# Batch 0 of a routed expert kernel: rows fetched by slot through a table made on TensorE, in place of rows scattered to their slots

## What is computed

```python
def _time_mix_layer(x, ln_w, ln_b, Wk, Wv, Wr, Wo):
    normed = _layer_norm(x, ln_w, ln_b)
    kv = (normed @ Wk.T) * (normed @ Wv.T)
    state = DECAY * state + (1.0 - DECAY) * kv_t          # along the tokens
    return x + (sigmoid(normed @ Wr.T) * states) @ Wo.T
x = _layernorm(x + attn(x))                               # two such layers
top_k_logits, expert_indices = top_k(x @ router_w + router_b, 2)
expert_inputs = zeros(E, cap, C).at[expert, pos].add(x)   # rows by slot
h = expert_inputs @ w_c_fc + b_c_fc;  g = expert_inputs @ w_gate + b_gate
o = silu(h * g) @ w_c_proj + b_c_proj
out = _layernorm(x + sum over k of prob[k] * o[expert[k], pos[k]])
```

## Time and profile before

| what | us |
|---|---|
| median of three timed runs | 365.52 (362.71 to 366.84) |
| span of the profiled execution | 382.6 |
| PE busy in it | 332.7 (87%) |
| DVE busy | 262.8 (69%) |
| POOL busy | 203.9 (53%) |
| ACT busy | 166.2 (43%) |

### The profile page before, as it was taken

How to read it: one execution, slowest core, us unless ns; L and a number is a source line. 1 busy time by engine, 2 the same in 40 slices (tenths; PEclk the granted TensorE clock), 3 DMA queues, 4 the chain that set the end, 5 groups by cost and what they waited for, 6 DMA issues and landing times.

```text
span 382.6 us, 7195 instructions
## 1 busy us (share of the span) xinstructions
PE 332.7 (87%) x2338; PEld 292.0 (76%) x2338; DVE 262.8 (69%) x853; ACT 166.2 (43%) x302; POOL 203.9 (53%) x244
## 2 busy tenths in 40 slices
PE   6889975869999999999999999877799986997880
PEld 3555653669879789997888999877689886987870
DVE  6688895787668868787787798831437684675225
ACT  2644434436545445555454445432435443363200
POOL 4185078850345642244557668377554437764752
PEclk9999896969999999999999999996999999898996
DMA  8949743150131133111114532222256111111152
GB/s 207 207 58 203 186 147 119 59 140 2 32 100 36 50 87 99 35 48 33 38 37 174 150 100 54 61 75 62 61 138 121 37 42 51 23 47 40 28 153 69
DMA packets 61246, 32.61 MB, mean 85 GB/s; under 512 B 15995, under 2 KB 58823, under 8 KB 61210
## 3 DMA queue, kind: packets, MB, share of 16 engines
q1 hardware_dynamic: 55322, 23.43, 25.3%
q0 software_dynamic: 4256, 7.94, 7.2%
q10 hardware_dynamic: 1632, 0.79, 0.7%
HBM read 19.01 MB, written 13.69 MB: 85 GB/s over the span
## 4 chain that ended last, share of the span: by engine, by line
PE 67%; issue 9%; DVE 8%; POOL 7%; another core or an unknown queue 3%; DMA 3%; ACT 3%; POOLq 0%; DVEq 0%; ACTq 0%
PE ps_o L795 20%; POOL slot_rows L1495 3%; PE pair0g L780 3%; PE pair0g L778 3%; PE pair1g L778 3%; PE bank L756 3%; PE bank L639 2%; PE pair1g L780 2%; PE bank L649 2%; PE pair0g L779 2%; PE bank L619 2%; PE pair1g L779 2%; PE bank L651 2%; PE pair1h L778 2%
## 5 line engine op out<-in xcount | busy, mean ns | idle before, releaser
L795 PE MATMUL ps_o<-proj_sb,hidden 128*104 128x128 f32 x768 | 99.7, 279 | 4.2 <-DVE o_sb L1311 2.1
L795 PEld LDWEIGHTS ps_o<-proj_sb,hidden 128*104 128x104 f32 x768 | 93.3, 175 | 5.8 <-issue 5.4
L1495 POOL DMA_INDIRECT slot_rows<-x_rows,row_to x64 | 72.5, 1133 | 45.1 <-DVE prod L1299 25.8
L1547 POOL DMA_INDIRECT picked<-expert_rows,row_from x48 | 49.9, 1039 | 37.4 <-DVE prod L1299 24.3
L984 ACT ACTIVATE gate_s<-pair0g,bgate_sb 128x308 f32<-128x308 f32 x64 | 33.1, 517 | 81.8 <-PE pair0g L780 52.7
L1299 DVE SCALAR_TENSOR_TENSOR prod<-pair1h,bfc_sb,gate_s 128x308 f32<-128x308 f32 x64 | 34.0, 532 | 32.3 <-ACT gate_s L984 17.7
L1299 DVE SCALAR_TENSOR_TENSOR prod<-pair0h,bfc_sb,gate_s 128x308 f32<-128x308 f32 x64 | 34.2, 534 | 26.4 <-ACT gate_s L984 11.8
L991 ACT ACTIVATE hidden<-prod 128x616 f32<-128x616 f32 x64 | 45.6, 712 | 7.7 <-DVE prod L1299 7.7
L984 ACT ACTIVATE gate_s<-pair1g,bgate_sb 128x308 f32<-128x308 f32 x64 | 33.0, 515 | 33.8 <-PE pair1g L780 22.2
L778 PE MATMUL pair1g<-slotT_hi,gate_hi 128*128 128x308 f32 x64 | 26.6, 416 | 10.0 <-DVE prod L1299 4.9
L1512 POOL DMA_INDIRECT returned<-o_sb,home x21 | 21.6, 1029 | 17.3 <-DVE prod L1299 11.2
(11 more groups left out here) (233 smaller groups left out, 773.0 us busy)
## 6 DMA issues: line engine op xcount, KB each, us to landing
slot_in<-slot_rows SPq DMA_DIRECT2D x20, 260.0 KB
expert_rows<-o_sb SPq DMA_DIRECT2D x24, 156.0 KB
x_in<-in_L_attn_h SPq DMA_DIRECT2D x4, 512.0 KB, 5.7
x_rows<-in_L_ffn_w_gate SPq DMA_DIRECT2D x8, 256.0 KB
x_rows<-in_L_ffn_w_c_fc SPq DMA_DIRECT2D x8, 256.0 KB
proj_sb<-in_L_ffn_w_c_proj SPq DMA_DIRECT2D x8, 256.0 KB, 5.3
out<-picked SPq DMA_DIRECT2D x12, 128.0 KB, 2.6
slot_rows<-slot_in SPq DMA_DIRECT2D x5, 260.0 KB, 7.2
```

The source lines that it names most:

```text
L795: mm = nc.tensor.matmul(ps_o[0:PART, P * part:P * part + P], hidden[:, e % 2, c, PART * part:PART * part + PART], proj_sb[:, e, c, :], sta ...
L1495: nc.gpsimd.indirect_dma_start(out=slot_rows, out_offset=bass.IndirectOffsetOnAxis(ap=row_to[:, c:c + 1], axis=0), in_=x_rows[:, b, c // K ...
L1547: nc.gpsimd.indirect_dma_start(out=picked[:, j, k, :], out_offset=None, in_=expert_rows[b % 2], in_offset=bass.IndirectOffsetOnAxis(ap=row ...
```

## The change

For batch 0 alone, the scatter and the load of slots are replaced:

- SP writes the normed rows of batch 0 to a DRAM tensor `first_rows` in two DMAs, behind the loads of `proj_sb`.
- DVE (stage `map`) splits `row_to` into a block (row / 128) and a lane (row mod 128) and compares both with constant number lists: `in_block`, 128x320, and four `in_lane`, 128x512 each. POOL (`weigh`) multiplies `in_block` by the token numbers, in two instructions. PE (`map`) multiplies `in_lane` with these, 16 matmuls of 128x40 in bfloat16 into `ps_o`: the token number of every slot. DVE (`picks`) adds the two halves of it into `slot_token`.
- POOL (`fetch`) gathers each of the five groups with four indirect DMAs of 128 rows of 512 bytes from `first_rows` into the ring `slot_in`, 20 DMAs in all. POOL gets four more small constants at the start.
- The first pair no longer waits for all of the head. `out` of batch 1's last step moves into period 0 behind the first pair; slot groups 1 and 2 are transposed at points 1 and 7; the splitting of the weights of experts 4 to 7 (`high`, `low`) moves from the head to points 1 to 14 of period 0; the stages of `..._ROUTE` and `..._MIX` come one point later in period 0, and so do the scatters of batch 1. Four filler matmuls are put ahead of `kvr` of batch 1's third step.

```diff
+SCALAR_FIRST = {0: [("added", 1, 3)], 1: [("high", 4, 0), ("high", 4, 1)], 3: [("high", 5, 0), ("high", 5, 1)],
+                8: [("high", 6, 0)], 9: [("high", 6, 1)], 11: [("high", 7, 0)], 13: [("high", 7, 1)]}
+VECTOR_FIRST = {0: [("stats", 1, 5)], 3: [("low", 4, 0), ("low", 4, 1), ("stats", 2, 0)],
...
+SLOT_TURNS_FIRST = {1: (0, 1), 7: (0, 2), 8: (0, 3), 19: (0, 4), 28: (1, 0), 29: (1, 1), 30: (1, 2)}
...
+def stages_at(table, b, point):
+    if later(b):
+        return table.get(point, [])
+    return table.get(point - 1, []) + (table.get(point, []) if point + 1 == POINTS else [])
...
+            for half in range(2):
+                sp.wait_ge(normed_made[1], step(0, 4 + half))
+                sp.dma_start(first_view[:, HT * half:HT * half + HT, :], x_ln[:, 0, HT * half:HT * half + HT, :])\
+                  .then_inc(first_stored, 16)
...
-            load_slots(0, range(GROUPS))
...
+            def slot_map(b, _):
+                pe.wait_ge(blocks_weighed, 2)
+                for c in range(K * TILES):
+                    if c % 4 == 0:
+                        pe.wait_ge(lanes_made, c // 4 + 1)
+                    mm = nc.tensor.matmul(ps_o[:, 0:2 * BLOCKS], in_lane[:, P * c:P * c + P],
+                                          weighed[:, c, :, :].rearrange("p w h -> p (w h)"),
+                                          start=(c == 0), stop=(c == K * TILES - 1))
...
                 if c == 0 and not later(b):
-                    for read in (r_copied, k_copied, kv_made):
+                    for read in (r_copied, k_copied):
                         pe.wait_ge(read, nth(1, 4, 4))
-                    pe.wait_ge(rows_made, 1)
-                    pe.wait_ge(pool_low_made, 2 * LOW_BY_POOL)
-                    pe.wait_ge(vector_low_made, 2 * (E - LOW_BY_POOL))
-                    pe.wait_ge(x_added, step(1, 3))
...
+                for i in range(4):
+                    nc.vector.tensor_tensor(in_lane[:, 4 * P * i:4 * P * i + 4 * P].rearrange("p (c l) -> p c l", l=P),
...
+                                            .to_broadcast([P, 4, P]), ALU.is_equal).then_inc(lanes_made, 1)
...
+            def fetch(b, g):
+                if g == 0:
+                    pool.wait_ge(map_copied, 2)
+                    pool.wait_ge(first_stored, 16 * 2)
+                    pool.wait_ge(rows_zeroed, 16 * GROUPS)
+                if g >= SLOT_RING:
+                    pool.wait_ge(slots_turned, g - SLOT_RING + 1)
+                for i in range(4):
+                    nc.gpsimd.indirect_dma_start(
+                        out=slot_x[:, g % SLOT_RING, i, :], out_offset=None, in_=first_rows,
+                        in_offset=bass.IndirectOffsetOnAxis(ap=slot_token[:, 4 * g + i:4 * g + i + 1], axis=0),
```

More of the change, by code:

```diff
@@ L106 @@
+FILL = {("weights", 0, 0): 12, ("turn", 0, 0): 1, ("turn", 0, 3): 3, ("turn", 0, 4): 6, ("turn", 0, 5): 2, ("count", 0, 0): 6,
+        ("kvr", 1, 2): 4}
 TENSOR_MIX = {9: [("turn", 0)], 10: [("kvr", 0)], 12: [("turn", 1)], 13: [("kvr", 1)], 14: [("out", 0)],
@@ L171, in scatters_at @@
         return [n for n in range(K * TILES) if SCATTER_FROM + 3 * n // 4 == point]
-    return [n for n in range(K * TILES) if SCATTER_FROM + n == point]
+    return [n for n in range(K * TILES) if SCATTER_FROM + n + (not later(b)) == point]
 def nth(b, per, k):
@@ L739, in turn_slots @@
                     pe.wait_ge(rows_made, b + 1)
-                if g == 2:
+                if g == 1 and not later(b):
+                    pe.wait_ge(k_copied, mixed - 1)
+                if g == 2 and later(b):
                     pe.wait_ge(kv_made, mixed)
@@ L743, in turn_slots @@
                     pe.wait_ge(logits_copied, nth(b, 2, 2))
+                if g == 2 and not later(b):
+                    pe.wait_ge(logits_copied, nth(1, 2, 2))
                 if g < 2 and later(b):
@@ L857, in period @@
                     hidden_pair(b, e, j)
+                    if not later(b):
+                        for name, of, n in TENSOR_FIRST.get(point, ()):
+                            stages[name](of, n)
                     if b == LAST:
@@ L1008, in period @@
                     gate_copy(b, e, j)
+                    if not later(b):
+                        for name, of, n in SCALAR_FIRST.get(point, ()):
+                            stages[name](of, n)
                     if b == LAST:
@@ L1414, in period @@
                     product(b, e, j)
-                    if point in SLOT_TURNS:
-                        ahead, g = SLOT_TURNS[point]
+                    if not later(b):
+                        for name, of, n in VECTOR_FIRST.get(point, ()):
+                            stages[name](of, n)
+                    if point in slot_turns(b):
+                        ahead, g = slot_turns(b)[point]
                         if b + ahead < B:
@@ L1532, in low_of @@
                                         ALU.subtract).then_inc(pool_low_made, 1)
-            stages = {"rstd": rstd_of, "shares": shares, "scatter": scatter_tile, "low": low_of}
+            stages = {"rstd": rstd_of, "shares": shares, "weigh": weigh, "fetch": fetch, "low": low_of}
             def gather(b, c):
```

188 lines of the change are left out of this document (132 added, 56 removed).

## The result

The changed kernel takes 373.62 us (median of 4, 371.59 to 376.05) against 366.18 of the kernel before, timed beside it on the same chip: a ratio of 1.0235, with a 95% interval of 1.0182 to 1.0287. I had predicted 364.5, within 1%, so the prediction is wrong in size and in sign. A second set of runs gives 372.98 and 1.0213 (1.0172 to 1.0253).

The account below looks back on a forecast made before the run. TensorE was taken to bound period 0, after a gap before its first pair. A 5.6 us earlier first pair, shrunk to 1.6 by DVE's queue, left 1.0: 365.5 - 1.0 = 364.5 us, range 360.0 to 368.6.

Parts of the forecast that it names:

- The table and fetches: Head: `kv` at 50.9, `weigh` 0.5 to 2 and hidden, gathers 1.45 each, group 0 issued at 60.8, needed at 73.
- Rival C: POOL: gathers cost 2.15, delaying the first pair and `rstd` of batch 2; slower by 4 to 5, 370; chance 0.08.
- The first pair, 76.85: End of the head: the first pair starts at 76.85, 5.6 earlier than 82.46, with DVE ending the wait.
- rival B: Low TensorE clock behind the gap 57.9 to 63.3: first pair 2 to 4 later, whole 366.5 to 368.5; chance 0.2.
- kvr (2.58 ...), to 69.1: TensorE in the head, behind `carry` and four fillers: `kvr` takes 2.58 and ends at 69.1.
- DVE from product 0 to product 9, 20.6: Period 0: 18.6 of DVE work plus 2 of waits, product 9 at 98.8; the lead shrinks from 5.6 to 1.6.
- From pair 8 on: Later period 0: pair 12 at 105.4 against 106.36, then TensorE has most to do; gain 0.9 to 1.
- The sum: Whole kernel: span 382.6 - 1.0 = 381.6, carried to the median as 365.5 - 1.0 = 364.5.
- Rival A: Period 0: DVE does not hold TensorE, pair 12 at 100.95; gain 5.4, 360.1; chance 0.24.
- the likeliest case: Period 0: DVE's queue holds TensorE with waits of 0 to 4; 362.5 to 366, chance 0.48.

Follow-up runs that it names:

- e9: e3 with both `rstd` ahead of the gathers, the slots' low part ahead of the head's last `stats`, only 4 fillers, ahead of the first pair: 362.14 us, ratio 0.9940.
- e1: Changed kernel plus 12 filler matmuls ahead of the transposes in the head and 10 ahead of the first pair: median 371.35 us, no ratio.
- e3: Changed kernel with the fillers of e1 and the early splits and statistics of e2: 364.79 us, ratio 1.0001 to the kernel before.
- e4: Kernel before with only the table, gathers and stores of rows in place of the scatters and load: 370.71 us, ratio 1.0154.
- e8: e4 with the `high` and `low` splits reordered, `high` of expert 4 behind `added` and `turned`: 368.41 us, ratio 1.0110.
- e10: Changed kernel, unchanged, run again with more rounds: 372.98 us, ratio 1.0213 to the kernel before.
- e5: Changed kernel with only the two `stats` of batch 2's first step moved to the head: 370.42 us, ratio 1.0132.
- e6: Changed kernel with only expert 4's split (two `high`, two `low`) moved to the head: 369.99 us, ratio 1.0114.
- e2: Changed kernel with expert 4's split and the two `stats` of batch 2's first step both moved to the head: 368.41 us, ratio 1.0114.

## Why the prediction was wrong, by its steps

- **The table and fetches.** Right in its times, in part by luck. `kv` was expected at 50.9 and started at 50.73, `picks` ended in time, and no transpose waited for a gather. But `weigh` took 3.1 (48.25 to 51.39), over its bound of 2, and TensorE waited 0.93 for it; nothing came of that, because `picks` stands behind the scan. The 23.1 us for 15 scatters are 1.54 each, not the 1.45 taken; gathers came every 1.30, except behind a slow one. That group 0 was issued by 60.65 (60.8 forecast) is the sum of one gather of 2.07 and three of 1.00. Rival C did not come: no `norm` waited behind the last eight gathers. Its second half was hardly tested here, since DVE came to `norm` of batch 2 only at 106.28, with `rstd` ready at 98.4; once the rest is faster it shows (0.36 in e9). The first gather started 0.27 within a scan; of the others four took 1.16 to 1.53, one of them (1.53) started within a `low`, and a gather that started with a scan (72.16, the scan at 72.15) took 1.00. For C, 0.7 would have been needed on each of 20; in all the twenty took 22.2 where 20 times 1.00 is 20. The rule of the Trainium skill (SBUF — State Buffer, "Who interferes with whom"), that a VectorE instruction with two SBUF inputs contends with a GpSimd instruction that reads SBUF, agrees with the two slowest of these and not with the one at 72.16.

```profile
L1646 POOL DMA_INDIRECT slot_in<-first_rows,slot_token x20: 992/999/2072, 54.7 to 96.0; - x20
```

- **The first pair, 76.85.** Measured 80.28. `norm` started at 62.12 as forecast (62.15); then the granted clock was 0.50 over the `carry`, the fillers and part of `kvr`. That is rival B, with its place and its price (2 to 4 us later, 79 to 81). The fillers show it: without the cold stretch 3.0 us come back. Counted from `row_to`, the first pair was forecast 29.1 behind and came 33.0 behind; of the 0.9 that the clock does not explain, half lies ahead of `norm` and half behind it. The step that failed is "kvr (2.58 ...), to 69.1" at full clock: the prediction had the half-clock stretch behind the old gap in its rows, saw the new gap, and still gave this 0.2.

- **DVE from product 0 to product 9, 20.6.** This is the step that turned a gain into a loss. Measured 26.59 (82.23 to 108.82). The work was counted right, the waits were not: one window over this stretch,

```profile
82.23:108.82 26.59, 21.09 (x148) 19.84 (x148) 18.61 (x83) 13.11 (x26) 12.53 (x16) 0.85 0.21 61
```

  has DVE busy for 18.61 us against 18.6 in the sum, and so 7.98 us of waiting where I took 2 and allowed 4. With the head's clock kept up (e1) it is 5.7, and with splits and `stats` early as well (e3) 3.3:

```profile
78.57:102.82 24.25, 18.75 (x146) 17.49 (x146) 18.51 (x83) 13.11 (x26) 12.53 (x16) 0.93 0.23 66
```

```profile
80.28:98.64 18.36, 16.69 (x146) 15.75 (x146) 15.05 (x64) 12.01 (x24) 12.44 (x16) 1.00 0.23 59
```

  So DVE's queue did not just hold TensorE: each held the other in turn, through the copy of the slots on ScalarE and through the bank of `logits`. The prediction added up one engine's queue and took the others' answers as ready.

- **From pair 8 on.** The prediction said that "the work done by then is the same in both" and gave the rest of the period no cost at all. Pairs 8 to 12 take 0.84 more, of which 0.56 is a wait for a product (at 108.36), and 12 to 32 take 1.46 more. It is almost the same in every version that keeps the change's order (11.07 for the first piece in e9, where POOL's `rstd` adds 0.36), and nothing in the two that have the old one (e4, e8). In e3 TensorE waits 0.63, 0.65 and 0.50 in the second piece, where before it waits 0.26 and 0.54. Which of the later stages, the splits of experts 6 and 7 or the shift by a point, makes these was not tried.

- **The sum.** Against the kernel before, pair 32 is 9.99 us later in the recorded profiles: first pair -2.58, pairs 0 to 6 +4.00, 6 to 8 +6.27, 8 to 12 +0.84, 12 to 32 +1.46. The timed medians differ by 7.4, as the profiled execution was the longest of its four (376.05). Of the 6.27, 1.6 went with the clock (11.03 to 9.42 in e10), 2.9 with the `stats` ahead of the first `top` (9.42 to 6.48 in e5, which takes away the wait of 1.88 and the low clock that e10 still has behind it), 0.9 with the splits (to 5.62), and 0.9 stays.

- **Rival A** is excluded: DVE held TensorE more than in the likeliest case.

The chance of a loss over 1% was 0.11, from C and the end of B. What was missed is that B does not stop at one place: behind the waits for DVE's queue the low clock came back, in this profile twice more (at the first pair and near 97), in e10 once, and each time it was added to the waits ahead of it.

## What to carry to other kernels

Closing a gap helps only if the work that lay in its shade has another place to go: count where each moved split or statistic lands, and let it land where its engine is idle, not where its queue feeds the bound one. When two engines feed each other point by point, walk the queue edge by edge (which bank, which copy, which small reader is behind the new instruction), since the sum of one engine's work was exact here and told only 18.6 of 26.6 us. Price every stretch in which TensorE idles with the low clock behind it, as a cost that comes with some chance, and put small instructions that others wait for (`rstd`) ahead of long runs of DMA issues (the head was 1.8 us shorter for it).

## What the runs showed of the hardware

The same gap does not always bring the low clock. Ahead of the first pair PE idled 2.57 in both profiles of the changed kernel, the same program: the mean clock from pair 0 to 6 was 0.89 in one and 1.00 in the other. Ahead of the transposes of `normed` PE idled 3.35 to 3.38 us in the changed kernel, in e10, e5, e6 and e2, and the clock fell to 0.50 in four of these and stayed at 1.00 in e2. The windows 66 to 68 of e10 and then of e2:

```profile
66.00:68.00 2.00, 2.00 (x12) 2.00 (x11) 1.55 (x4) 0.78 (x1) 1.70 (x2) 0.50 0.14 16
```

```profile
66.00:68.00 2.00, 2.00 (x12) 1.36 (x12) 2.00 (x6) 0.74 (x2) 2.00 (x1) 1.00 0.26 33
```

The Trainium skill (TensorE: Matmul & The Clock Gate, "What's actually happening") says that the watch over TensorE's activity runs freely and does not start with the kernel, so that where a change of clock falls varies. No run here shows that watch; that the place varies, the traces agree. Between a head in which the clock fell and one in which it did not lie 2.7 to 3.0 us. A profile of one execution therefore shows one draw of such a stretch.
